# Expert stage of an attention and mixture-of-experts chain: order of the splits in paired turns, eight result slots, and looser waits between scatter-adds

## The reference: what is computed

```python
gate_logits = xt @ Wg.T + bg              # 3584 tokens, 8 experts
w, idx = top_k(gate_logits, 2); w = softmax(w)
h = relu(W1[e] @ x + b1[e])               # 256 -> 512
y = W2[e] @ h + b2[e]                     # 512 -> 256
out[token] = x[token] + sum over its 2 experts of w * y
```

## Time and profile before

| | us |
|---|---|
| median of 3 runs | 1056.76 |
| profiled execution, its time | 1057.91 |
| its span, first to last instruction | 1056.0 |
| TensorE's weight loads of the expert stage begin (first paired turn) | 832.6 |
| first scatter-add begins | 850.5 |
| first scatter-add of a single (unit 48) begins | 1006.9 |
| last scatter-add (unit 62) begins | 1051.8 |

### The profile page before, as it was taken

One profiled execution on the slowest core, in us unless ns is written; L12 is line 12 of the kernel. 1 busy time (PEld: TensorE's weight loads), 2 busy tenths in 40 slices (PEclk: granted clock), 3 DMA queues, 4 the chain that ended last, 5 costly groups with the idle time before them and its releaser, 6 DMA issues. The chain is left out here.

```text
span 1056.0 us, 31314 instructions
## 1 busy us (share of the span) xinstructions
PE 954.6 (90%) x10664; PEld 664.5 (63%) x10664; DVE 751.6 (71%) x2101; ACT 544.9 (52%) x1068; POOL 552.6 (52%) x897
## 2 busy tenths in 40 slices
PE   4799999999999999988799999999975499999994
PEld 2466666666666666655456666666644377777884
DVE  4688888888888888884768888888854255555663
ACT  3566666666666666655224444444442145555541
POOL 6655554555545555410125777777776344445435
PEclk9999999999999999998799999999986599999997
DMA  5644344444344343322275556655561356765544
GB/s 154 175 137 136 104 123 121 136 111 122 118 129 137 109 125 112 114 80 83 73 196 168 183 184 192 190 182 184 179 197 55 98 123 160 167 164 88 93 68 52
DMA packets 107276, 140.54 MB, mean 133 GB/s; under 512 B 23929, under 2 KB 92592, under 8 KB 106928
## 3 DMA queue, kind: packets, MB, share of 16 engines
q1 hardware_dynamic: 94594, 121.38, 38.9%
q0 software_dynamic: 12528, 17.18, 8.8%
HBM read 93.38 MB, written 38.35 MB: 125 GB/s over the span
## 5 line engine op out<-in xcount | busy, mean ns | idle before, releaser
L996 DVE TENSOR_REDUCE smax<-psum 112x2 f32<-112x750 f32 x240 | 221.3, 934 | 44.7 <-PE psum L448 42.0
L828 ACT ACTIVATE probsT<-psum 125x896 f32<-125x896 f32 x173 | 158.8, 918 | 54.1 <-PE psum L463 52.5
L2013 POOL DMA_INDIRECT out_dram<-y,token_at x63 | 98.7, 1567 | 118.7 <-DVE y L2184 89.5
L2173 DVE TENSOR_TENSOR h_lo<-h,h_hi 128x512 f16<-128x512 f32 x63 | 43.2, 686 | 64.8 <-ACT h_hi L2129 55.5
L1719 DVE SCALAR_TENSOR_TENSOR acc<-psum,neg_bias,acc 128x448 f32<-128x448 f32 x112 | 75.8, 679 | 10.6 <-PE psum L1542 9.7
L483 PE MATMUL psum<-probsT,v_aug 125*32 125x112 f32 x2688 | 81.6, 262 | 0.0
L448 PE MATMUL psum<-k_stack,q_stack 63*128 63x375 f16 x480 | 78.4, 326 | 3.5 <-DVE smax L996 0.7
L2141 ACT ACTIVATE h<-psum,b 128x256 f32<-128x256 f32 x96 | 40.3, 471 | 79.4 <-PE psum L2041 76.8
L1461 POOL DMA_INDIRECT dispatch_dram<-rows,slots_at x64 | 64.1, 1002 | 28.5 <-issue 28.5
L1542 PE MATMUL psum<-xT_hi,we_hi 128*128 128x448 f16 x256 | 70.2, 356 | 1.1 <-ACT we_hi L1641 1.1
L463 PE MATMUL psum<-q_stack,k_stack 64*128 64x112 f16 x1384 | 64.2, 212 | 6.4 <-DMA q_stack<-neg_max 1.6
(11 more groups left out here) (299 smaller groups left out, 2460.6 us busy)
## 6 DMA issues: line engine op xcount, KB each, us to landing
k_stack<-k_hi_dram SPq DMA_DIRECT2D x64, 188.0 KB, 2.7
we<-in_ctxT_dram SPq DMA_DIRECT2D x32, 375.0 KB, 3.7
ctxT<-in_ctxT_dram SPq DMA_DIRECT2D x32, 375.0 KB
ctx_rows<-in_ctx_dram SPq DMA_DIRECT2D x32, 375.0 KB
w_raw<-in_w_dram SPq DMA_DIRECT2D x32, 256.0 KB, 3.9
rows_e<-dispatch_dram SPq DMA_DIRECT2D x24, 272.0 KB
k_hi_dram<-k_hi SPq DMA_DIRECT2D x32, 188.0 KB, 3.0
k_lo_dram<-k_lo SPq DMA_DIRECT2D x32, 188.0 KB, 3.3
```

Of the source, the lines that this page charges most:

```text
L828: nc.scalar.activation(probsT[:, p, c, hg, :, :, :].rearrange("p k h q -> p k (h q)"), psum[0:KC, 0:2, 0:4 * S], ACT.Exp, scale=float(HD) ...
L996: nc.vector.reduce_max(smax[:, (u - LAG_B) % 2, 2 * (s % 4) + s // 4::PAIRS], psum[0:S, pair_bank(s):pair_bank(s) + 2, 0:KV], AX.X).then_i ...
L2013: nc.gpsimd.indirect_dma_start(dram["out"], bass.IndirectOffsetOnAxis(token_at[:, unit // PAIR % ROW_TURNS, unit % PAIR:unit % PAIR + 1], ...
```

## The change

1. In paired turns ScalarE makes `x_hi` of the next turn right after the relus, ahead of `h_hi` of unit 0; VectorE makes `x_lo` ahead of `h_lo` of unit 0. Turns of singles keep their order.
2. `y` has 8 slots and 8 semaphores `added`, and the token indices are kept for 6 turns.
3. GpSimd waits otherwise: always for the scatter-add of the unit four before (`UNORDERED`); where a unit is the first of a pair or a single, also for the three before, but from unit 17 on to a value from the table that is met only late where the unit begins an expert. Units up to 16 that begin a pair always wait for all before them. At each looked-up wait a semaphore `passed` that nobody reads is raised.

```diff
+SLOTS = 8
...
-    SLOTS = 4
-    FREE_FROM = SLOTS + 1
+    TOKEN_TURNS = SLOTS // PAIR + 2
+    FREE_FROM = 2 * SLOTS + 1
+    UNORDERED = 4
...
-    token_at = sb("token_at", [128, ROW_TURNS, PAIR], U32)
+    token_at = sb("token_at", [128, TOKEN_TURNS, PAIR], U32)
...
                 follows = paired(unit // PAIR) and unit % PAIR > 0
-                if not follows:
-                    before = look_up(pool, 2, unit, 16, landed(NU)) if unit >= FREE_FROM else landed(unit - 1)
+                chosen = not follows and unit >= FREE_FROM
+                if chosen:
+                    less = look_up(pool, 2, unit, 16, landed(NU))
+                    full = less + 16
+                if chosen:
+                    for k in range(1, UNORDERED):
+                        pool.wait_ge(added[(unit - k) % SLOTS], full if landed(unit - k) == landed(unit - 1) else less)
+                    pool.sem_inc(m["passed"], 1)
+                elif not follows:
+                    for k in range(1, min(UNORDERED, unit + 1)):
+                        pool.wait_ge(added[(unit - k) % SLOTS], landed(unit - k))
+                if unit >= UNORDERED:
+                    pool.wait_ge(added[(unit - UNORDERED) % SLOTS], landed(unit - UNORDERED))
                 wait(pool, m["y_rdy"], unit + 1)
-                if unit > 1:
-                    pool.wait_ge(added[(unit - 2) % SLOTS], landed(unit - 2))
-                if unit > 0 and not follows:
-                    pool.wait_ge(added[(unit - 1) % SLOTS], before)
...
-                high_h(n, 0)
+                if not paired(n):
+                    high_h(n, 0)
                 if n + 1 < TURNS:
                     high_x(n + 1)
                     e = look_up(act, 0, PAIR * (n + 1), 0, E - 1)
+                if paired(n):
+                    high_h(n, 0)
...
-                low_h(n, 0)
+                if not paired(n):
+                    low_h(n, 0)
                 if n + 1 < TURNS:
                     low_x(n + 1)
+                if paired(n):
+                    low_h(n, 0)
...
-        "unit_before": 16 * np.floor((unit_no - 1) / 4),
+        "unit_before": 16 * (np.floor((unit_no - 1) / SLOTS) - 1),
```

More of the change, by code:

```diff
@@ L1930, in expert_phase @@
         hhi_rdy0 hhi_rdy1 hlo_rdy0 hlo_rdy1 down_done0 down_done1 y_sum_rdy0 y_sum_rdy1 y_rdy
-        token_rdy added0 added1 added2 added3""".split()
+        token_rdy added0 added1 added2 added3 added4 added5 added6 added7""".split()
     m = {n: sem("x_" + n) for n in names}
@@ L2005, in _ @@
                 follows = paired(unit // PAIR) and unit % PAIR > 0
-                if not follows:
-                    before = look_up(pool, 2, unit, 16, landed(NU)) if unit >= FREE_FROM else landed(unit - 1)
-                wait(pool, m["y_rdy"], unit + 1)
-                if unit > 1:
-                    pool.wait_ge(added[(unit - 2) % SLOTS], landed(unit - 2))
-                if unit > 0 and not follows:
-                    pool.wait_ge(added[(unit - 1) % SLOTS], before)
-                nc.gpsimd.indirect_dma_start(dram["out"], bass.IndirectOffsetOnAxis(token_at[:, unit // PAIR % ROW_TURNS, unit % PAIR:unit % PAIR + 1], 0),
+                chosen = not follows and unit >= FREE_FROM
[11 more added lines that the diff above has]
+                    pool.wait_ge(added[(unit - UNORDERED) % SLOTS], landed(unit - UNORDERED))
+                wait(pool, m["y_rdy"], unit + 1)
+                nc.gpsimd.indirect_dma_start(dram["out"], bass.IndirectOffsetOnAxis(token_at[:, unit // PAIR % TOKEN_TURNS, unit % PAIR:unit % PAIR + 1], 0),
                                              y[:, unit % SLOTS, :], None, compute_op=ALU.add).then_inc(added[unit % SLOTS], 16)
@@ L2189, in tokens @@
                 wait(dve, rows_in[n % ROW_TURNS], rows_arrived(n))
-                nc.vector.tensor_copy(token_at[:, n % ROW_TURNS, 0:len(units(n))].rearrange("p (n o) -> p n o", o=1),
+                nc.vector.tensor_copy(token_at[:, n % TOKEN_TURNS, 0:len(units(n))].rearrange("p (n o) -> p n o", o=1),
                                       rows[:, n % ROW_TURNS, 0:len(units(n)), AT_TOKEN:AT_TOKEN + 1]).then_inc(m["token_rdy"], 1)
```

## The result

The changed kernel takes 1040.43 us in the median of 4 runs (1038.13 to 1042.37). The kernel before, run beside it, takes 1057.16 (four runs in all, 1054.79 to 1062.4). The ratio is 0.9837, with a 95% interval of 0.9803 to 0.9871. The forecast was 1039, in a range from 1034 to 1050. The profiled execution took 1042.37 us, with a span of 1040.1 against 1056.0.

The account below looks back on a forecast made before the run. TensorE was taken as the bound up to about unit 46, then GpSimd with its DMAs. -15.8 (splits) - 3.5 (singles' waits) + 0.8 (added waits) = -18.5 us from 1057.9 gave 1039 us, range 1034 to 1050.

Parts of the forecast that it names:

- The splits: Paired turns: `x_lo` starts 0.66 us earlier in 24 turns, 15.8 us saved, bounds 7.7 to 18.2.
- The second hole: Idle TensorE weight loads after one chunk of `up_pair`, 0.68 us a turn on average; predicted to shrink by 0.34.
- the first hole: Idle TensorE weight loads between the second layer's last load and `up_pair`'s first, 0.32 us a turn; predicted to close.
- The tail: Scatter-adds of the singles: looser GpSimd waits save 3.5 us, more waits per single cost 0.8.
- the added waits: Six serial steps among the singles get about three more sequencer operations each at 0.04 us: +0.8 us, at most 2.9.
- GpSimd's lag at the front: Paired units up to 16: 7.0 us per pair, GpSimd 10 us late after 8 pairs, cost taken as 0.
- The chain at the end: Last stretch of the changed profile: the chain of waits still made of landings from unit 46 or 47 on.
- The port: VectorE's `y` writes beside GpSimd's scatter-adds: taken as 0; the skill page's lock would add an estimated 5 us.
- Only the first hole closes: Rival, paired turns: the look-up takes its time whatever `x_lo` does; 7.7 for 15.8, 1047 us, up to 1050; chance 0.20.
- The tail gives nothing back: Rival, tail: landings lengthen and waits cost their upper bound, or GpSimd's lag reaches VectorE; 1044 us; chance 0.07.
- scatter-adds in a queue: Rival, tail: beyond two in flight the DMA queue serves additions singly; 1061 to 1072 us; chance 0.04 with other slowdowns.
- The splits do nothing: Rival, paired turns: fixed-length sequencer address work bounds `up_pair`'s start; only the tail's 2.7 us remain, 1054 us; chance 0.07.

Follow-up runs that it names:

- ScalarE alone: The kernel before with `x_hi` ahead of `h_hi` on ScalarE in paired turns, VectorE's order left old: 1061.22 us in one run.
- both halves together: The changed kernel, 1.63%; its halves on the kernel before: new split order alone 1042.16 us (1.5%), new waits with eight slots alone 1054.31 us (0.24%).
- the look-up moved: TensorE's look-ups of the next expert moved behind the second layer, ahead of the `xlo_rdy` wait: 1032.65 us in the changed kernel, 1046.16 us in the kernel before.
- the copies later: The changed kernel with SyncE's copies of the singles' weights within SBUF issued five turns later: 1036.03 us in one run.

## Why the prediction was right, and where it was not

**The bound** was read rightly. "Both holes hang on the end of `x_lo`" is shown three ways: it gets later and the turn longer (ScalarE alone), the look-up leaves the hole and the hole closes, and both halves together give the gain. That the sequencer stands at the wait for `xlo_rdy` explains why a load that takes 0.30 us and needs nothing of `x_lo` was on the path.

**The splits: -15.8 predicted, -13.0 at unit 46.** Three steps of the term were off, the first against the other two.

- *The shift of `x_lo`.* It came 0.78 us earlier in the mean and not 0.66: `x_hi` starts 0.11 before the second relu ends (906.54 against 906.65), the 0.1 that I had kept as an upper bound.
- *The second hole.* The term took every 0.01 of `x_lo` as 0.01 of turn, with the look-up's length unchanged. But the look-up went from 0.39 us to 0.55 in the mean of turns 3 to 24. In the 15 turns with SyncE's copies it had begun 2.2 us (median) behind the issue of the second one and took 0.43; now it begins 0.6 to 1.4 us behind it and takes 0.65. One of them, the copy's issue and then the look-up, in the turn with the hole of 0.34:

```profile
901.14 0.53 SPq L1996 DMA_DIRECT2D spare_w<-w_lo  x1
```

```profile
L1951 PEldq TENSOR_LOAD <-table x1: 614/614/614, 902.5 to 902.5; - x1
```

- *What a hole is worth.* With no hole a turn is 5.68 (the look-up moved), so 1.00 us of holes made the turn only 0.83 longer (6.51). So each of the two costs 0.08 less than its length. The rows fit: a product begins 0.11 us behind its own weight load as a rule, so it has one more to run when the loads stop, and right behind a hole (902.07 and 902.08) only 0.01. Tried on the others: the changed kernel has 6.5 / 22 = 0.30 us a turn, in a hole in 17 of 22 turns, 5.68 + 0.30 - 0.08 x 17 / 22 = 5.92, against 5.92 measured; the kernel before with the look-up moved has one of 6.9 / 22 = 0.31 in each, 5.68 + 0.31 - 0.08 = 5.91, against 5.92. So the closing of the first hole (0.32) gave less than 0.32.

Then the count. I took 24 turns of 0.66. Turns 2 to 24 gave 12.8 of 14.5. Turns 0 to 2 gave 1.7; the granted clock fell there in both profiled executions alike (842 to 846 us: 0.59 before, 0.57 after), so it is not the clock's. And the last stretch gives back 0.8: `x_lo` has moved 0.78 ahead within its turn and the work behind unit 46 has not, so it is 9.4 us from the one to the other and not 8.6.

**The tail: -2.7 predicted, -3.0 measured.** Units 57 to 62 came at GpSimd's pace and 54 and 55 too. For the added waits 0.8 was taken, as three more operations of the sequencer in each of six steps. The traces show one: the waits are folded into `L2015`, and only `L61`, the wait for `y_rdy`, is new behind the landing. From the end of the landing wait to the scatter-add it is 0.75 us in each of five steps before (to units 49 to 52 and 56) and 0.85 in each of them now: 0.10 a step, 0.6 for six. The size was near by luck of two errors, three times too many operations at under half of what one costs. 46 to 52 took 26.87 and takes 27.08; over all kernels it is 26.9 to 27.9 with the old waits and 26.5 to 27.6 with the new, so that stretch can't show it. The Trainium skill, Advanced Engine Details and Errata, Network/Comms, with its 50 to 100 ns for each semaphore read, gave an estimate of 0.9 to 1.8 us for 18 operations; with the six that there are it would give 0.3 to 0.6, an estimate again, and the measured 0.10 a step lies at its upper end.

**GpSimd's lag at the front** was put at 7.0 us a pair and 10 us after eight pairs, and its cost at nothing. The scatter-adds of units 2 to 16 start 6.33 us apart by pairs in the mean, and that of unit 16 began 3.0 us after its `y` (898.32 to 901.29). The cost was right, the lag three times too long.

**Eight slots "is what allows the next gain" was wrong.** With four, the gain is there. The new rule itself always waits for the unit four before, so it never has more than four scatter-adds in flight, which is what four slots hold.

**The chain at the end** was to be made of landings from unit 46 or 47 on. The view of the chain seems to deny it, as it stops at 1024.82:

```profile
1024.82 0.36 DVE y L2196
1025.18 0.02 issue
1025.20 0.02 POOLq L61
```

But that is a wait put down to the wrong event. The `y` is that of unit 61, while `L61` asks for the `y` of unit 57, done at 1016.28. By the starts, the steps to units 49 to 52 and to 56 are landings still, each begun 0.85 us behind the end of its landing wait; only from 56 to 62, and in 53 to 55, is it GpSimd's own work on one scatter-add after another.

**The port.** The 5 us that the Trainium skill, SBUF — State Buffer, SBUF: two separate sides, would have made of it are not there: the 63 scatter-adds took 1554 to 2004 ns with a median of 1560, against 1554 to 1985 and 1558. But the prediction's "the median nothing" looked at the wrong engine. It is VectorE's `y` that gets longer, and only beside a scatter-add. The second row below lies within the first:

```profile
1013.80 2.00 POOL L2022 DMA_INDIRECT out_dram<-y,token_at  x1 [3.23 <-DMA out_dram<-y,token_at]
...
1014.91 0.49 DVE L2196 TENSOR_SCALAR y<-y_sum,rows_e 128x256 f32<-128x256 f32 x1 [0.20 <-issue]
```

Over all eleven kernels the 415 writes of `y` that overlap no scatter-add took at most 0.36 us; of the 278 that overlap one, 39 took over 0.40, up to 0.70. In the changed kernel 7 of 26 did, up to 0.63. None of it is on the path here. Which of the two stretches the other, and whether that page's lock is the reason, no run shows.

**The rivals.** *Only the first hole closes* is refuted: over the paired turns the holes fell from 21.9 to 6.5 us, by more than twice what the first one holds (22 x 0.32 = 7.0). *The tail gives nothing back* and *scatter-adds in a queue* are refuted by tails of 48.3 to 50.0 us in five kernels with the new waits, against 52.1 to 53.3 in six with the old; the landing's median went from 4.4 to 4.1 us and its longest from 5.4 to 6.4 (of the 16 and 24 landings that these two traces hold). *The splits do nothing* is refuted by the kernel that has only them.

**The sum.** -18.5 was 2.8 too much for the splits (0.7 of it because the stage began that much later) and 0.3 too little for the tail; the span fell by 15.9. The median differs from the forecast by only 1.4 us because the profiled execution of the changed kernel, 1042.37 and 3.0 above the 1039.4 of the sum, was the longest of its four runs.

## What to carry to other kernels

Where a sequencer waits for a late operand, everything behind that wait in program order starts late, register loads and address work too; look for what could stand ahead of the wait before making the operand earlier. Here moving a look-up of 0.30 us took 1.0% off the kernel before and 0.7% more off the changed one, where the reordering of two engines took 1.5% alone. By the turn (6.51 before) each of the two makes 5.92 and both together 5.68: they share the second hole, so they add only in part. In the profiled execution 4 us of what the look-up alone gained were lost again to scatter-adds that had fallen behind: a bound that was idle before can eat a gain once the turns get shorter. A hole in the weight loads is worth a little less than its length, and a looser wait needs no more buffers unless a trace shows who would fill them.

## What the runs showed of the hardware

- **A look-up is slow just behind a copy within SBUF.** Over the changed kernel, the one before and seven of the experiments (all but those with the look-up moved), a TensorE look-up that began 0.5 to 2 us behind the end of a copy's issue took 0.67 us in the mean (74 of them), 2 to 2.5 us behind it 0.42 (50), and with no copy in the 3 us before it 0.32 (211, of which 21 took over 0.40, at most 0.64). The longest was 1.07. Why is open; that they share a path to SBUF would fit and was not tried.
- **The clock at the stage's start.** In the first turns the products pause, and afterwards the granted clock either stays at full (2.4 GHz) or falls to half (1.2 GHz) for some microseconds. It fell in the changed kernel, where the products were busy for 1.20 of 3 us and then 842 to 846 us has a mean of 0.57. It did not with the copies later, in whose trace 1.82 of 4 us were busy:

```profile
839.00:842.00 3.00, 1.20 (x8) 0.51 (x7) 1.95 (x4) 2.13 (x5) 0.00 (x0) 0.97 0.00 0
842.00:846.00 4.00, 3.96 (x21) 3.10 (x22) 0.02 (x1) 1.13 (x3) 0.00 (x0) 0.57 0.00 0
846.00:849.00 3.00, 3.00 (x30) 2.70 (x29) 1.93 (x4) 2.08 (x5) 0.00 (x0) 1.00 0.00 0
```

```profile
834.00:838.00 4.00, 1.82 (x16) 1.35 (x16) 1.97 (x4) 2.08 (x5) 0.00 (x0) 1.00 0.00 0
838.00:846.00 8.00, 8.00 (x75) 7.26 (x74) 3.48 (x8) 5.03 (x12) 1.99 (x2) 1.00 0.06 11
```

  It makes 1.9 us in `x_lo` of turn 0 to 2 (14.65 against 12.78) for the same order of work; a comparison of single runs carries that with it. In all it fell in seven of the eleven profiled runs, that of the kernel before among them, and not in those of the splits alone, of ScalarE's order alone, of the look-up moved in the changed kernel, and of the copies later. What decides it is open.
- **GpSimd's own pace**, with all waits met: one scatter-add of 128 rows in 1.87 us (units 56 to 62), of which 1.56 is GpSimd's own operation.
- **`y` beside a scatter-add**: the same VectorE operation takes 0.35 to 0.36 us alone and up to 0.70 beside one (see the port).
